# Every second message's low half made on GpSimd, and one slot instead of two gathered beside each message

## The reference

```
m = (embedding @ W_msg.T + b_msg).reshape(n, 4, 128)     # a message per node and edge type
r = segment_sum(m[src, etype], dst)                      # summed at the target node
embedding = gru_cell(r, embedding)                       # four steps of this
```

## Time and profile before

| what | value |
|---|---|
| median of 3 runs (lowest to highest) | 2268.68 us (2268.68 to 2269.72) |
| the profiled execution's own time | 2271.41 us |
| span of its trace | 2269.6 us |
| PE busy over the span | 2067.3 us, 91% |
| DVE busy | 1346.3 us, 59% |
| ACT busy | 495.6 us, 22% |
| POOL busy | 888.6 us, 39% |
| mean granted clock of PE, as a share of 2.4 GHz | 0.926 |

### The profile page before, as it was taken

The page is one execution under the profiler, slowest core; times in us unless marked ns, Lnnn a source line. Parts: engine busy times, 40 slices in busy tenths (PEclk is TensorE's granted clock), DMA queues, the critical chain, the costliest instruction groups (busy, mean ns, idle before and its releaser), DMA issues.

```text
span 2269.6 us, 42977 instructions
## 1 busy us (share of the span) xinstructions
PE 2067.3 (91%) x15410; PEld 1445.6 (64%) x16017; DVE 1346.3 (59%) x2875; ACT 495.6 (22%) x1130; POOL 888.6 (39%) x1022
## 2 busy tenths in 40 slices
PE   3666664899999999999999999999999999999998
PEld 2333332898998988989755576555665556655576
DVE  8989898776776768776853235532355323553233
ACT  4989898200000000000221012110122101220001
POOL 4877775000000000000038870388703887038870
PEclk9655555799999999999999999999999999999999
DMA  2000001000000000001531110311103111033111
GB/s 82 24 35 24 35 23 46 31 2 2 2 1 2 1 2 1 1 2 61 150 108 41 42 40 23 109 42 42 40 23 109 42 42 40 22 110 70 42 40 30
DMA packets 62750, 89.94 MB, mean 40 GB/s; under 512 B 31953, under 2 KB 48927, under 8 KB 59654
## 3 DMA queue, kind: packets, MB, share of 16 engines
q1 hardware_dynamic: 21185, 54.88, 7.3%
q0 software_dynamic: 38400, 31.28, 5.9%
q10 hardware_dynamic: 2944, 0.93, 0.2%
HBM read 47.48 MB, written 39.05 MB: 38 GB/s over the span
## 4 chain that ended last, share of the span: by engine, by line
PE 75%; DVE 15%; issue 4%; DVEq 2%; ACT 2%; POOL 0%; POOLq 0%; DMA 0%; ACTq 0%
PE ps L917 39%; PE ps L1021 28%; PE ps L900 4%; DVE marks L1224 3%; DVE m_full L1699 2%; DVEq L1211 2%; DVE m_parts L1692 2%; PE ps L798 1%; PE ps L931 1%; DVE dig L1252 1%; DVE big L1254 1%; PE ps L880 1%; PE ps L842 1%; PE ps L1006 1%; DVE hot_pair L1226 1%
## 5 line engine op out<-in xcount | busy, mean ns | idle before, releaser
L508 POOL DMA_INDIRECT big<-messages_by_edge_kind,edge_row x480 | 616.9, 1285 | 1167.3 <-issue 886.4
L917 PE MATMUL ps<-slots,m_parts 125*128 125x436 fp8e4 (+1 forms) x5600 | 960.7, 329 | 4.5 <-DVE m_parts L1692 3.2
L917 PEld LDWEIGHTS ps<-slots,m_parts 125*128 125x128 f16 x5600 | 540.5, 98 | 360.1
L1021 PE MATMUL ps<-parts,big 125*128 125x256 f16 x6125 | 673.0, 273 | 6.7 <-issue 3.9
L1021 PEld LDWEIGHTS ps<-parts,big 125*128 125x128 fp8e4 x6125 | 592.8, 98 | 64.9
L1530 DVE TENSOR_SCALAR slots<-big 128x1400 int32<-128x1400 int32 (+1 forms) x224 | 196.5, 920 | 258.9 <-PE ps L917 258.8
L798 PE MATMUL ps<-hot_pair,weighed 125*128 125x228 f16 x1000 | 218.3, 370 | 130.3 <-ACT weighed L621 72.0
L798 PEld LDWEIGHTS ps<-hot_pair,weighed 125*128 125x128 f16 x1000 | 117.5, 123 | 230.9 <-ACT weighed L621 191.8
L621 ACT ACTIVATE weighed<-marks,win_w 125x128 f16<-125x128 f16 x625 | 194.7, 391 | 51.3 <-DVE marks L1224 51.0
L560 ACT ACTIVATE rs<-rs 125x25 f32<-125x25 f32 (+3 forms) x5 | 1.1, 216 | 707.4 <-DVE rs L1094 707.4
L1719 DVE SCALAR_TENSOR_TENSOR gate_r<-ps,over,gate_r 128x436 f32<-128x436 f32 (+2 forms) x32 | 20.0, 624 | 213.7 <-PE ps L900 211.8
(11 more groups left out here) (231 smaller groups left out, 1542.6 us busy)
## 6 DMA issues: line engine op xcount, KB each, us to landing
messages_by_edge_kind<-m_parts SPq DMA_DIRECT2D x20, 1120.0 KB
packed_counts<-packed SPq DMA_DIRECT2D x16, 625.0 KB, 2.9
big<-messages_by_edge_kind,edge_row POOLq DMA_INDIRECT x480, 3.3
big<-packed_counts SPq DMA_DIRECT2D x4, 1400.0 KB, 6.4
big<-packed_counts SPq DMA_DIRECT2D x3, 1050.0 KB, 5.8
messages_by_edge_kind<-m_parts SPq DMA_DIRECT2D x20, 130.0 KB
hd<-in_x SPq DMA_DIRECT2D x1, 1562.5 KB
x_again<-in_x SPq DMA_DIRECT2D x1, 1562.5 KB
```

Of the source, the lines that this page charges most:

```text
L508: pool.indirect_dma_start(out=picked[0:CH, r, w, :, :].rearrange("p h f -> p (h f)"), out_offset=None, in_=m_dram[:, :], in_offset=bass.In ...
L917: last = pe.matmul(ps[:, k % 2, 0:SIZES[k] * QD], m_parts[0:Q, a, t, h, :], slots_f8[0:Q, t % 2, 0:SIZES[k], a, 0:QD], start=a == 0 and t ...
L1021: last = pe.matmul(ps[:, n % RING, 0:2 * F], tot_f8[0:Q, c, a, :], both((parts0, parts1)[par], a), start=a == 0, stop=a == TILES - 1)
```

## The change

Three things are edited. `LAG` goes from 21 to 0: beside a message PE gathers only type 0 (two matmuls), and type 1 of all 25 tiles, 50 matmuls, follows after the last message. The low halves of tiles 7, 9, ..., 23 are made by POOL (`LOWS_POOL`), with a semaphore of their own, `message_parts_of_gpsimd`; DVE keeps the low halves of the other 16 tiles. And every wait on low halves is split in two, one for each maker: on PE ahead of a gather, on DVE ahead of a bias (the buffer `a % 2` is free when the low half of `a - 2` is made, by whichever engine), and on SP ahead of a store, whose loop over the steps is written out now. The arithmetic is the same.

```diff
--- before.py
+++ after.py
@@ -66,7 +66,9 @@
 AHEAD = 6
 EARLY = 4
 LEAD = 4
-LAG = 21
+LAG = 0
+LOWS_POOL = list(range(AHEAD + 1, TILES, 2))
+LOWS_DVE = [a for a in range(TILES) if a not in LOWS_POOL]
 RING = 5
 PS0 = 12
 DIGITS = 5
@@ -329,6 +331,7 @@
         s_nrm, s_ntr, s_emb = sem("normed_made"), sem("normed_transposed"), sem("embedding_made")
         s_slot, s_slot_free = sem("slot_unpacked"), sem("slot_used")
         s_m, s_mfull, s_hi, s_mp = sem("messages_made"), sem("messages_copied"), sem("high_parts"), sem("message_parts")
+        s_mp_p = sem("message_parts_of_gpsimd")
         s_dm, s_dmr = sem("largest_degree_made"), sem("largest_shared")
         s_rt, s_rl = sem("messages_summed"), sem("messages_summed_low")
         s_grz, s_gn, s_sig, s_ct, s_tanh = sem("rz_products"), sem("n_products"), sem("rz_gates"), sem("n_sum"), sem("candidate")
@@ -337,6 +340,13 @@
         s_ld, s_sacc, s_epi = sem("tile_loaded"), sem("tile_summed"), sem("tile_finished")
         s_ld_m, s_sacc_m, s_epi_m = sem("typed_tile_loaded"), sem("typed_tile_summed"), sem("embedding_tile_made")
         s_x2b, s_otr, s_res, s_out = sem("x2_back"), sem("embedding_back"), sem("result_made"), sem("out_stored")
+
+        def wait_parts(eng, s, a):
+
+            eng.wait_ge(s_mp, len(LOWS_DVE) * s + sum(n <= a for n in LOWS_DVE) + 1)
+            own = sum(n <= a for n in LOWS_POOL)
+            if own:
+                eng.wait_ge(s_mp_p, len(LOWS_POOL) * s + own)
 
         def turn_places(what, i):
             if what == "dense":
@@ -410,9 +420,9 @@
                     sp.dma_start(big1[:, a:z].rearrange("p (b n) -> p b n", b=NBD),
                                  packed_dram[:, 0:NBD, START[k] * TILES * BQ:(START[k] + SIZES[k]) * TILES * BQ]).then_inc(s_pblk[k], 16)
                     store_x2(k)
-                with sp.Fori(0, STEPS) as s:
+                for s in range(STEPS):
                     for first, last in STORED:
-                        sp.wait_ge(s_mp, TILES * s + last + 1)
+                        wait_parts(sp, s, last - 1)
                         for lo, hi in ((0, ROWS_A), (ROWS_A, Q)):
                             sp.dma_start(m_dram.rearrange("(p a t) f -> p a (t f)", a=TILES, t=TYPES)[lo:hi, first:last, :],
                                          m_parts[lo:hi, first:last, :, :, :].rearrange("p a t h f -> p a (t h f)")).then_inc(s_mst, 16)
@@ -499,6 +509,10 @@
                 share_largest()
                 pool.wait_ge(s_rows, 1)
                 for s in range(STEPS):
+                    for a in LOWS_POOL:
+                        pool.wait_ge(s_hi, TILES * s + a + 1)
+                        pool.tensor_tensor(m_parts[0:Q, a, :, 1, :], m_full[0:Q, a % 2, :].rearrange("p (t f) -> p t f", f=F),
+                                           m_parts[0:Q, a, :, 0, :], ALU.subtract).then_inc(s_mp_p, 1)
                     pool.wait_ge(s_mst, 16 * 2 * len(STORED) * (s + 1))
                     for lot in range(LOTS):
                         r = lot % SHELVES
@@ -950,7 +964,10 @@
                                 message_when_ready(s, a + AHEAD)
                             elif 2 * (AHEAD - LEAD) <= a < TILES - LEAD:
                                 message_when_ready(s, a + LEAD)
-                            wait_alone(s_mp, TILES * s + a + 2)
+                            if a in LOWS_POOL:
+                                wait_alone(s_mp_p, len(LOWS_POOL) * s + LOWS_POOL.index(a) + 1)
+                            else:
+                                wait_alone(s_mp, len(LOWS_DVE) * s + LOWS_DVE.index(a) + 2)
                             gather(s, k, (0, 1) if a < LAG else (0,), a)
                         for a in range(LAG, TILES):
                             gather(s, k, (1,), a)
@@ -1692,18 +1709,29 @@
                 TT(m_parts[0:Q, a, :, 1, :], m_full[0:Q, a % 2, :].rearrange("p (t f) -> p t f", f=F), m_parts[0:Q, a, :, 0, :],
                    ALU.subtract).then_inc(s_mp, 1)
 
-            def bias(s, a):
-
-                dve.wait_ge(s_mp, TILES * s + max(a, 1))
+            def bias(s, a, parts_free):
+
+                parts_free(s, a)
                 dve.wait_ge(s_m, TILES * s + a + 1)
                 STT(out=m_full[0:Q, a % 2, :], in0=ps[0:Q, 6 + a % 2, :], scalar=1.0 / EMB, in1=bias_msg[0:Q, :],
                     op0=ALU.mult, op1=ALU.add).then_inc(s_mfull, 1)
 
-            def messages(s, first, last):
+            def two_engines(s, a):
+
+                if a >= 2 and a - 2 in LOWS_POOL:
+                    dve.wait_ge(s_mp_p, len(LOWS_POOL) * s + LOWS_POOL.index(a - 2) + 1)
+                else:
+                    dve.wait_ge(s_mp, len(LOWS_DVE) * s + max(sum(n <= a - 2 for n in LOWS_DVE) + 1, 1))
+
+            def one_engine(s, a):
+
+                dve.wait_ge(s_mp, TILES * s + max(a, 1))
+
+            def messages(s, first, last, parts_free=two_engines):
 
                 for a in range(first, last):
-                    bias(s, a)
-                    if a > first:
+                    bias(s, a, parts_free)
+                    if a > first and (parts_free == one_engine or a - 1 in LOWS_DVE):
                         low(s, a - 1)
                 low(s, last - 1)
 
@@ -1775,7 +1803,7 @@
                         elif more_steps:
                             unpack(s, BLOCKS, 1)
                             for a in range(EARLY, AHEAD):
-                                bias(s + 1, a)
+                                bias(s + 1, a, two_engines)
                             meanwhile = lambda: low(s + 1, EARLY)
                         else:
                             add_results((3, 4))
@@ -1822,7 +1850,7 @@
                 steps_g.base, steps_g.k = steps_g.base + steps_g.k, 0
                 start = steps_g.base
                 with dve.Fori(0, STEPS) as s:
-                    messages(s, 0, TILES)
+                    messages(s, 0, TILES, one_engine)
                     with dve.Fori(0, TILES) as c:
                         steps_g.base, steps_g.k = start + 4 * (TILES * s + c), 0
                         sum_low(TILES * s + c, ps[:, 0, 0:Q], r_parts[:, 0, 1, 0:Q], r_parts[:, 0, 0, 0:Q])
```

## The result

The changed kernel takes 2308.95 us (median of 4 runs, 2308.47 to 2309.54), the kernel before 2268.68 us on the same chip: 1.0178 times as long, with a 95% interval of 1.016 to 1.0195: under 2%, and far outside the scatter of the executions. The forecast was 2295 us with a range of 2281 to 2313. The direction and most of the mechanism came out as forecast; some 11 us of the 40 come from a place at which the prediction did not look. The profiled execution took 2308.85 us with a span of 2307.3 us; the spans differ by 37.7 us.

A forecast was written before the change was run, and what follows sets the result against it. PE and DVE were taken as level, so only PE's gaps could be won back. 24.6 us for the steps plus 1.6 for the clock made 26.2, hence 2295 us against a median of 2268.7; range 2281 to 2313.

The forecast's parts named there:

- What bounds the kernel: Second layer's four steps: PE and DVE are level at 1.41 us a tile; a faster DVE can return only PE's gaps.
- PE's side: Message part: 42 matmuls a step move behind the messages; cover is lost at the start, the end grows by 7.33 us.
- The start gap: PE's wait for the bias of tile 6 at the message part's start: from 1.90 to 3.39 us.
- POOL's loop: Odd tiles' buffer, bias to high half to POOL's low half to next bias: 1.51 + L, 2.68 us a pair.
- L: Time of POOL's subtraction for one low half: estimated 1.17 us, between 0.87 and 1.47.
- The clock: PE's clock may fall at the message part's start: 0 to 0.9 us a step, 0.4 taken, 1.6 in all.
- What costs nothing: POOL's idle time, the stores, the split waits on PE, DVE and SP, and SP's written-out loop: no cost.
- The sum: Bias 7 to type 2: 34.73 us a step, 24.6 more over four steps, plus 1.6 for the clock: 26.2.
- POOL at twice DVE: Rival: POOL's low half takes 1.38 us, a pair 2.89; 2302 us in all; chance 25%.
- Shutting out: Rival: POOL's subtraction keeps DVE from starting a bias, a pair takes 3.29 us; 2313 us; chance 12%.
- Even: Rival: with POOL's subtraction at 0.53 us or less its loop hides; 4.1 us more, 2273 us; chance 6%.
- Stores and gathers: Message stores end some 1.4 us earlier; indirect DMAs follow as before, and slack covers a store held up by POOL.

The follow-up runs named there:

- moved by 50: The changed kernel with 50 DVE waits that are always met put ahead of the loop over steps; 2298.44 us, 1.0133 times before.
- the third buffer: The changed kernel with those 50 DVE waits and a third buffer for the fp32 message from tile 6 on; 2278.45 us, 1.0034 times before.
- `LAG = 4`: The changed kernel with 50 always-met DVE waits, the second slot of tiles 0 to 3 left beside the messages; 2287.98 us, 1.008 times before.
- `LAG = 18`: The changed kernel with 50 always-met DVE waits and two buffers, 14 instead of 50 matmuls moved behind the messages; 2270.30 us, 1.0005 times before.

## Why the prediction was right, and where it fell short

**What bounds the kernel.** Right. PE and DVE are level: POOL's low halves alone come to 0.9997, and by them steps 0 and 2, in which the clock holds, are 0.8 us shorter than before.

**PE's side.** Right in both terms. The start gap, 3.39 forecast from the earlier trace rows, is 3.34 to 3.43 us in steps 1 to 3 where no stall lies on it (2.60 in step 0); the tail is 52 matmuls in one piece. The moved matmuls alone cost 29.1 us against their own before (2268.17).

**POOL's loop.** Right. L is 1.156 (forecast 1.17), a pair 2.71 us (2.68). In step 0, the only one at full clock, it is 35.06 us from bias 7 (1130.98 + 1.28 - 0.69 = 1131.57) to type 2 (1156.92 + 52 x 0.187), where the working gave 34.73:

```profile
1130.98 1.28 DVE L1716 SCALAR_TENSOR_TENSOR m_full<-ps,bias_msg 125x512 f32<-125x512 f32 x2
```

```profile
1156.92 15.41 PE L931 MATMUL ps<-slots,m_parts 125*128 125x436 fp8e4 x82 [0.36 <-DVE m_parts L1709]
```

**The clock.** Too small. In steps 1 to 3 the same stretch takes 35.78, 36.01 and 35.94 us, so 0.7 to 0.95 each, 2.55 together; 0.4 a step, 1.6 in all, was forecast. That the clock makes this difference is shown by step 0 itself: in the changed kernel moved by 50 it did fall there, and the same stretch takes 35.95 us (1131.42 to 1157.65 + 52 x 0.187), 0.9 more. "About even" was too low a chance: of the 12 starts of steps 1 to 3 in the four runs with `LAG = 0` it fell at 10 (behind 3.3 to 3.4 us, or 8.9 with the stall).

**What costs nothing.** Here the prediction failed. "The two waits in place of one on PE, DVE and SP stand at the same places" asks only who waits for whom. By the traces DVE's loop loses nine low halves and one semaphore instruction and gains 23 that work on registers, from which the waits take their values. It is 13 longer in all and ends at another place; that was not weighed, and the term stood at nothing. It brought 10.9 us of stall at two branches, 10.5 by the run without it. At another place of the loop the same 13 cost nothing, and no row of before had a price for them; that the loop would grow could be read from the code.

**The sum.** From bias 7 to type 2 the four steps take 142.79 us, 114.33 before: 28.5 more, where 24.6 + 1.6 = 26.2 were forecast. With the stall 39.4, less the 1.5 us by which step 0 began earlier in this execution (bias 7 at 1131.57 against 1133.09): 37.9, against 37.7 between the spans. So the forecast of 2295 was some 2 us low by its own terms and 11 by the one that it did not have. That 2309 stands within 2281 to 2313 is partly luck: the forecast's own range ended at 2307, and what lay above it was there for two rivals that did not come true. Without the stall the time is 2298.44, which the mechanism and the sum give to within 4 us.

**The rivals.** POOL at twice DVE: no, 1156 / 682 ns is 1.70 times. The factor of 1.96 from the Trainium skill, GPSIMD Engine Reference, Performance versus the Vector engine (the page has it for 2048 columns of fp32) is not borne out at this shape. Shutting out: no; a bias on DVE takes 0.69 us beside POOL's subtraction, as without it. This subtraction runs beside the bias that starts at 1434.92 (DVE's timeline above):

```profile
1434.94 1.16 POOL L514 TENSOR_TENSOR m_parts<-m_full,m_parts 125x512 f16<-125x512 f32 x1 [1.56 <-ACT m_parts L705]
```

That DVE's low halves, with both inputs in SBUF, would run beside it too is not shown: none of them overlaps it by more than 0.05 us.

Even: no, L is not 0.53; but with the third buffer, which takes POOL out of the loop, the pair has the 2.04 us of that rival, and the time comes to 2278.45 where that rival had 2273. The time that came, 2309, lies between two of the rivals and is neither of them.

**Stores and gathers.** Right that nothing is lost here: PE waits for gathered rows in neither kernel. POOL's wait for the stores is shorter than in the earlier trace rows, but that comes of its waiting for ACT's high halves first (969.9 us in its row above). The last low half itself starts, counted from bias 6, 0.1 to 1.05 us earlier than before in steps 0 to 2 and 0.55 us later in step 3, where 1.4 us earlier was forecast:

```profile
POOL big L522 <- DMA messages_by_edge_kind<-m_parts: 28.5, 4, 7.3
```

## What to carry to other kernels

Where two engines are level, taking work from one shows little until the other's gaps are closed; look for the buffer that ties a helper into the loop before judging the helper by its speed. An edit that adds instructions within a loop of an engine's program can cost by where the loop then lies: look for idle time named "issue" at the branch back, and move the loop by instructions that cost nothing to tell place from work. A range that holds the time is no proof of the sum: look in the trace for every term. Matmuls moved out from beside waiting work give up cover at one end and stand bare at the other, and a clock that falls in the new gap adds to it.

## What the runs showed of the hardware that was not expected

A branch back on DVE cost 4.1 us (a body of 290 instructions) and 5.45 us (303) in two places of the loop, and nothing in two others, with the same work in it. POOL's subtraction of 512 columns per partition, fp32 and fp16 in, fp16 out, took 1.156 us where DVE took 0.682, and DVE's biases stayed at 0.69 us beside it. The granted clock fell to 0.50 behind gaps of 3.3 to 3.4 us in most step starts, but not in step 3 of the run with the moved matmuls alone, nor in step 3 with three buffers. Behind a gap of 1.94 us in step 1 it fell with `LAG = 4` and with POOL's low halves alone, and did not with `LAG = 18`; behind 2.60 us in step 0 it fell in the changed kernel moved by 50 and not in the changed kernel itself. So in these runs the length of the gap alone does not say whether the clock falls.
